# State stage of an audio tower: the cap of the inverse decays and the zeroing of first decays move from VectorE to GpSimd

## The chip, the cores and the metric

The kernel runs on one core of a Trainium2 chip. The metric is the device time in microseconds (us) of one execution; the time of a kernel is the median of several runs. Lines named L1033 and so on are lines of the kernel before.

## The reference, cut to what matters

The model takes 32 sequences of 750 samples with 64 channels and cuts each into 92 patches of 128 features (2944 tokens in all). Then follow a state space layer with a memory read-out, a mixture of six experts, a windowed attention and a second mixture. The change lies in the state space layer:

```python
delta = jnp.minimum(jax.nn.softplus(x_ssm @ delta_W + delta_b), 0.5)
A_cont = -jnp.exp(A_log)
DeltaA = delta[..., None] * A_cont
A_bar = jnp.clip(jnp.exp(DeltaA), 0.0, 1.0)
injection = jnp.where(jnp.abs(A_cont) > 0.0001, jnp.expm1(DeltaA) / A_cont, delta[..., None])
B_cont = jax.nn.silu(x_ssm @ B_W + B_b).reshape(Bsz, Tlen, d_h, n)
B_cont = 0.5 * (B_cont - jnp.mean(B_cont, axis=(0, 1), keepdims=True))
B_bar = jnp.nan_to_num(injection * B_cont, nan=0.0, posinf=1000.0, neginf=-1000.0)
A_shift = jnp.concatenate([jnp.ones((Bsz, 1, d_h, n), x_seq.dtype), A_bar[:, :-1]], axis=1)
pps = jnp.exp(jnp.cumsum(jnp.log(jnp.maximum(A_shift, 1e-06)), axis=1))
h_seq = jnp.cumsum(B_bar * pps, axis=1) / pps
C_coeff = jax.nn.silu(x_ssm @ C_W + C_b).reshape(Bsz, Tlen, d_h, n)
h_out = jnp.einsum('btdn,btdn->btd', h_seq, C_coeff)
```

There are 128 channels with 16 states each. The cumulative sum divided by the cumulative product is a recurrence, h[t] = h[t-1] / A_shift[t] + B_bar[t], and that is how the kernel computes it. The inverse decay 1 / A_shift is the growing exponential of the delayed delta, capped at 1e6, the inverse of the lower bound 1e-6; at the first token of a sequence it is set to zero, so that one scan can run over all 32 sequences.

## The kernel before, in words

The kernel has five stages. In each, every engine runs an instruction list of its own, the lists meet at semaphores, and every stage ends with all engines waiting for each other. The order of the work on each engine is written out by hand.

The second stage, the state stage, handles the 16 states one after another, in eight pairs (`NPAIR`). All its large tiles are 128 channels by `TOK` = 2944 tokens, `L` = 92 tokens to a sequence. Two slots u = 0 and 1 alternate for the buffers `bufB`, `bufC`, `th` and `ra`; `ea` exists once. For state n:

- ScalarE, `decays` (L745 on): `tanh` (L751) of half the decay's exponent into `th`; `exp_minus` (L756), the falling exponential, into `ea`; `exp_plus` (L761), the growing one, into `ra`. `exp_plus` of state n waits until the scan of state n-2 has released `ra` in its slot (`ra_free`). The order of a pair is tanh, exp_minus, exp_plus, tanh, exp_plus, exp_minus.
- TensorE, `states` (L1539 to L1541): the projections B and C of the state, three passes for each of eight banks of PSUM, 48 matmuls a state. The eight banks hold either B or C, so each group of banks must be emptied before the next can be filled.
- ScalarE, `silus`: the B group (L784) empties the banks into `bufB` and sums for the mean; the C group (L791) empties them into `bufC`. Before a C group it waits until the transfer of the state two before, which reads the same `bufC`, has landed (`Y_added`).
- VectorE, `injection` (L1028): `(ea + 1) * th`. `decay` (L1033, L1035): the cap of `ra` at 1e6 and the memset of every 92nd column to zero. `drive` (L1045, L1047, L1049): the mean of B, then `(B - mean) * th` into `bufB`. `recur` (L1054): the scan over `ra` and `bufB`. `read_out` (L1059): h times C into `bufC`. `weights_lo` (L1039), once a pair: the low part of the next weights.
- GpSimd, `add_state` (L601): a transfer that adds `bufC` to `Y` in place, for states 0 to 13; GpSimd then waits until it has landed. TensorE adds states 14 and 15.

VectorE's order in a pair is drive, scan, read_out of the first state, weights_lo, drive and scan of the second; then injection and decay for the first state of the next pair, read_out of the second, injection and decay for the second state of the next pair. SyncE loads the weights of each pair. The ScalarE side of the hand-over is:

```python
def exp_plus(n, u):
    wait_apart(act, ra_free, n + 1)
    act.activation(ra[:, u], dl[:, 0:TOK], ACT.Exp, scale=A_pos[:, bass.ds(n, 1)])\
        .then_inc(ra_ready, 1)
```

and the wait of a C group for the transfer:

```python
if not first:
    act.wait_ge(Y_added, 16 * n - 16)
```

Of the kernel before, what the change touches and what calls it, by code (L numbers as in the profile page):

```python
# [7 lines left out]
def audio_tower(nc, t, out):  # L8
# [11 lines left out]
    ALU = mybir.AluOpType  # L20
# [3 lines left out]
    B, L, D = out.shape  # L24
# [4 lines left out]
    TOK = B * L  # L29
    G = L + 1  # L30
    NS = 16
# [30 lines left out]
    with ctx:  # L62
# [3 lines left out]
        def sem(name):  # L66
            return ctx.enter_context(nc.semaphore(name))
# [48 lines left out]
        def take(*shape, parts=128):  # L116
            n = 1
            for s in shape:
                n *= s
            view = R[0:parts, taken[0]:taken[0] + n]  # L120
            taken[0] += n
            assert taken[0] <= R_COLS
            if len(shape) > 1:
                ax = "abcd"[:len(shape)]
                view = view.rearrange("p (" + " ".join(ax) + ") -> p " + " ".join(ax),
                                      **{x: s for x, s in zip(ax, shape)})
            return view
# [19 lines left out]
        def wait_apart(eng, s, value):  # L147


            eng.wait_ge(s, value)  # L150
            eng.sem_inc(apart, 1)
# [23 lines left out]
        def stage_end(eng, k):  # L175

            eng.drain().then_inc(stage_done, 1)  # L177
            eng.wait_ge(stage_done, 4 * k)
# [126 lines left out]
        ra = take(2, TOK)  # L305
        dl = take(1 + TOK)
        wBC = sb("wBC", [128, 2, 2, D])
        NPAIR = NS // 2
# [15 lines left out]
        Y_zero, Y_added = sem("Y_zero"), sem("Y_added")  # L324
        th_ready, ea_ready, ra_ready = sem("th_ready"), sem("ea_ready"), sem("ra_ready")
        th_free, ea_free, ra_free = sem("th_free"), sem("ea_free"), sem("ra_free")
        B_free = sem("B_free")
        prod_ready = sem("prod_ready")
        skip_mm = sem("skip_mm")

# [229 lines left out]
        def _(pool):  # L560
            step = Tally(pool, pool_step)
# [34 lines left out]
            pool.memset(Y[:, :], 0.0).then_inc(Y_zero, 1)  # L596
            pool.wait_ge(Y_zero, 1)

            def add_state(n, u):
                wait_apart(pool, prod_ready, n + 1)  # L600
                pool.dma_start(Y[:, :], bufC[:, u], accum_op=ALU.add, max_dma_last_dim=TOK // 2 * 4)\  # L601
                    .then_inc(Y_added, 16)
                pool.wait_ge(Y_added, 16 * n + 16)

            with pool.Fori(0, NPAIR - 1) as i:
                for u in range(2):
                    add_state(i * 2 + u, u)
            stage_end(pool, 2)

            def rstd_c(c):  # L610
# [318 lines left out]
        def _(dve):  # L929
            step = Tally(dve, dve_step)  # L930
# [93 lines left out]
            def injection(n, u):  # L1024

                dve.wait_ge(th_ready, n + 1)
                dve.wait_ge(ea_ready, n + 1)
                dve.scalar_tensor_tensor(th[:, u], ea, 1.0, th[:, u], ALU.add, ALU.mult).then_inc(ea_free, 1)  # L1028

            def decay(n, u):  # L1030

                dve.wait_ge(ra_ready, n + 1)
                step.add(dve.tensor_scalar(ra[:, u], ra[:, u], 1e6, None, ALU.min))  # L1033
                step.wait()
                step.add(dve.memset(ra[:, u, 0:TOK:L], 0.0))  # L1035

            def weights_lo(i, s):
                dve.wait_ge(w_hi_ready, i + 1)
                dve.tensor_tensor(w_lo[:, s], wBC[:, :, :, :], w_hi[:, s].bitcast(f32), ALU.subtract)\  # L1039
                    .then_inc(w_split, 1)  # L1040

            def drive(n, u):

                dve.wait_ge(bc_free, NH + (n * 2 + 1) * NH)
                step.add(dve.reduce_sum(mean[:, u:u + 1], part[:, u, :], axis=AX))  # L1045
                step.wait()
                step.add(dve.tensor_scalar(mean[:, u:u + 1], mean[:, u:u + 1], 1.0 / TOK, None, ALU.mult))  # L1047
                step.wait()
                dve.scalar_tensor_tensor(bufB[:, u], bufB[:, u], mean[:, u:u + 1], th[:, u],  # L1049
                                         ALU.subtract, ALU.mult).then_inc(th_free, 1)  # L1050

            def recur(n, u):
                dve.wait_ge(th_free, 2 + n + 1)
                dve.tensor_tensor_scan(bufB[:, u], ra[:, u], bufB[:, u], 0.0, ALU.mult, ALU.add).then_inc(ra_free, 1)  # L1054

            def read_out(n, u):
                dve.wait_ge(ra_free, 2 + n + 1)
                dve.wait_ge(bc_free, NH + (n * 2 + 2) * NH)
                step.add(dve.scalar_tensor_tensor(bufC[:, u], bufB[:, u], A_c[:, bass.ds(n, 1)], bufC[:, u],  # L1059
                                                  ALU.mult, ALU.mult))  # L1060
                step.wait()
                dve.sem_inc(B_free, 1)
                dve.sem_inc(prod_ready, 1)  # L1063

            def pair(i, s, more=True, weights=True):
                n = i * 2
                drive(n, 0)
                recur(n, 0)
                read_out(n, 0)
                if weights:  # L1070
                    weights_lo(i + 1, s)
                drive(n + 1, 1)
                recur(n + 1, 1)
                if more:
                    injection(n + 2, 0)
                    decay(n + 2, 0)
                read_out(n + 1, 1)
                if more:
                    injection(n + 3, 1)
                    decay(n + 3, 1)  # L1080

            dve.sem_inc(w_split, 1)
            weights_lo(0, 0)
            injection(0, 0)
            decay(0, 0)
            decay(1, 1)
            injection(1, 1)
            pair(0, 1)
            for i in step.loop(NPAIR // 2 - 1, 2 * (2 * 2 + 2 * 3)):
                pair(i * 2 + 1, 0)  # L1090
                pair(i * 2 + 2, 1)
            pair(NPAIR - 1, 0, False, False)
# [832 lines left out]
```

## Time and profile before

| what | value |
|---|---|
| median of 3 runs | 988.57 us (987.64 to 989.6) |
| the profiled execution's own time | 989.3 us |
| its span in the profile | 987.4 us |
| busy: TensorE, VectorE, ScalarE, GpSimd | 686.1, 673.5, 489.3, 279.8 us |
| state stage, VectorE busy from 113 to 432 us | 292.84 of 319.00 us |
| state stage, ScalarE busy from 113 to 432 us | 265.97 of 319.00 us |
| TensorE's granted clock from 148.85 to 378.52 us | 0.76 of full speed |

The profile counts an engine as busy while an instruction of its executes. Register, branch and semaphore instructions don't count. In brackets behind a row of the timeline stands how long the engine had been idle before the instruction, and what released it. [...]

### The profile page before, as it was taken

To read this page: it belongs to the slowest core of one execution; us is meant where nothing else is said; L and a number is where in the kernel's file an instruction comes from. 1 tells how busy PE (TensorE), PEld (TensorE's weight loads), DVE (VectorE), ACT (ScalarE), POOL (GpSimd) and SP (SyncE) were. 2 spreads that over 40 slices of the span, in tenths; PEclk is the share of its full clock that TensorE was granted. 3 is DMA by queue.
4 is the path that set the end of the run, shared out by engine and by line. 5 is a ranking of instruction groups with operands and counts; after the bars stand their busy time and mean duration, and the time that the engine had idled before them with its cause. 6 is when DMAs were issued, how large, how long until landed. Compare 5 with 4: busy or idle time off the path is not lost. (4 is left out here: it accounts for less than half of the span.)

```text
span 987.4 us, 12125 instructions
## 1 busy us (share of the span) xinstructions
PE 686.1 (69%) x3064; PEld 510.5 (52%) x3065; DVE 673.5 (68%) x1482; ACT 489.3 (50%) x691; POOL 279.8 (28%) x266
## 2 busy tenths in 40 slices
PE   6964253663753753856424993669999799999986
PEld 3542253563752743734322772346666566666654
DVE  0886379999999999968831442656857567675641
ACT  1234799889888988603211331234534344453432
POOL 0343101000000000002872442144352515445342
PEclk9995677877876777878556996779989989998999
DMA  4300425533543553316011211000000000000000
GB/s 163 128 5 0 160 72 98 107 61 79 109 77 72 96 98 61 61 34 229 22 34 32 60 54 56 22 0 1 9 1 8 2 8 0 8 9 0 8 3 14
DMA packets 22412, 50.97 MB, mean 52 GB/s; under 512 B 4485, under 2 KB 14704, under 8 KB 22016
## 3 DMA queue, kind: packets, MB, share of 16 engines
q0 software_dynamic: 6752, 24.53, 12.7%
q1 hardware_dynamic: 15616, 25.96, 8.4%
q8 instruction: 15, 0.25, 0.1%
q14 instruction: 29, 0.24, 0.1%
HBM read 24.44 MB, written 10.10 MB: 35 GB/s over the span
## 5 line engine op out<-in xcount | busy, mean ns | idle before, releaser
L1539 PE MATMUL psum<-s_xn_lo,s_split_hi 128*128 128x368 f32 x256 | 100.5, 393 | 148.0 <-ACT s_R L784 100.4
L1539 PEld LDWEIGHTS psum<-s_xn_lo,s_split_hi 128*128 128x128 f32 x256 | 59.1, 231 | 153.6 <-ACT s_R L784 102.8
L880 ACT ACTIVATE s_R<-psum,s_cols 128x368 f32<-128x368 f32 x96 | 54.2, 571 | 120.2 <-PE psum L1710 114.7
L1716 PE MATMUL psum<-s_R 128*128 128x368 f32 (+1 forms) x288 | 106.6, 491 | 0.0
L1054 DVE TENSOR_TENSOR_SCAN s_R<-s_R 128x2944 f32<-128x2944 f32 x16 | 100.7, 6291 | 0.6
L1540 PE MATMUL psum<-s_xn_hi,s_split_lo 128*128 128x368 f32 x256 | 96.9, 379 | 0.0
L1541 PE MATMUL psum<-s_xn_hi,s_split_hi 128*128 128x368 f32 x256 | 96.3, 376 | 0.0
L601 POOL DMA_DIRECT2D s_xnfm<-s_R x14 | 17.1, 1218 | 270.9 <-DVEq L1063 270.9
L1708 PE MATMUL psum<-s_xn_lo,s_split_hi 128*128 128x368 f32 (+1 forms) x144 | 78.7, 547 | 1.2 <-ACT s_R L880 0.9
L662 POOL TENSOR_TENSOR s_R<-s_R 128x368 f32<-128x368 f32 x48 | 46.5, 968 | 86.8 <-DVE s_R L1332 82.5
L1422 DVE TENSOR_TENSOR s_R<-psum,s_R 128x344 f32<-128x344 f32 x168 | 37.5, 280 | 44.4 <-PE psum L1782 42.1
L1716 PEld LDWEIGHTS psum<-s_R 128*128 128x128 f32 (+1 forms) x288 | 53.6, 195 | 25.4 <-issue 1.4
L791 ACT ACTIVATE s_R<-psum,s_cols 128x736 f32<-128x736 f32 x64 | 55.7, 877 | 14.9 <-PE psum L1541 10.3
L1540 PEld LDWEIGHTS psum<-s_xn_hi,s_split_lo 128*128 128x128 f32 x256 | 59.0, 230 | 0.0
L685 POOL TENSOR_TENSOR s_R<-s_R 128x368 f32<-128x368 f32 x48 | 46.5, 968 | 43.1 <-DVE s_R L1422 34.1
L1541 PEld LDWEIGHTS psum<-s_xn_hi,s_split_hi 128*128 128x128 f32 x256 | 58.2, 227 | 0.0
L1028 DVE SCALAR_TENSOR_TENSOR s_R<-s_R 128x2944 f32<-128x2944 f32 x16 | 51.4, 3214 | 9.2 <-ACT s_R L756 6.9
L784 ACT ACTIVATE s_R<-psum,s_cols 128x736 f32<-128x736 f32 x64 | 55.7, 876 | 2.3 <-PE psum L1541 1.2
L1059 DVE SCALAR_TENSOR_TENSOR s_R<-s_R,s_A_c 128x2944 f32<-128x2944 f32 x16 | 52.6, 3285 | 2.1 <-DVE s_R L1054 1.3
L1049 DVE SCALAR_TENSOR_TENSOR s_R<-s_R,s_mean 128x2944 f32<-128x2944 f32 x16 | 52.6, 3285 | 0.6
L1740 PE MATMUL psum<-s_R 128*112 128x368 f32 x112 | 45.7, 500 | 7.0 <-DVE s_R L1361 6.6
L761 ACT ACTIVATE s_R<-s_R,s_A_pos 128x2944 f32<-128x2944 f32 x16 | 43.9, 2742 | 13.0 <-DVE s_R L1054 13.0
(228 smaller groups left out, 1623.2 us busy)
## 6 DMA issues: line engine op xcount, KB each, us to landing
s_xnfm<-s_R POOLq DMA_DIRECT2D x14, 1472.0 KB, 10.5
s_R<-in_xg SPq DMA_DIRECT2D x8, 744.0 KB, 4.2
x_sorted<-in_x_init SPq DMA_DIRECT2D x1, 5082.0 KB, 18.7
s_R<-in_w SPq DMA_DIRECT2D x2, 1536.0 KB, 9.8
s_wBC<-in_wBC SPq DMA_DIRECT2D x8, 256.0 KB, 2.8
s_R<-x_sorted SPq DMA_DIRECT2D x28, 66.0 KB, 1.8
s_R<-y_rows SPq DMA_DIRECT2D x8, 184.0 KB
out<-s_R SPq DMA_DIRECT2D x8, 184.0 KB
```

The costliest lines, as they stand in the source:

```text
L784: act.activation(group(bufB, u, h), psum[:, h * HB:(h + 1) * HB, 0:CT], ACT.Silu, bias=cols[:, bass.ds(n + at["B_b"], 1)], scale=1.0, accu ...
L791: act.activation(group(bufC, u, h), psum[:, h * HB:(h + 1) * HB, 0:CT], ACT.Silu, bias=cols[:, bass.ds(n + at["C_b"], 1)], scale=1.0).then ...
L880: act.activation(fh[0:kk, e % 3, j], bank(j % 2 if e % 2 == 0 else (j + 1) % 2, kk), ACT.Gelu, bias=col("b1", 2 * e + j) if j < 2 else b1b ...
L1028: dve.scalar_tensor_tensor(th[:, u], ea, 1.0, th[:, u], ALU.add, ALU.mult).then_inc(ea_free, 1)
L1049: dve.scalar_tensor_tensor(bufB[:, u], bufB[:, u], mean[:, u:u + 1], th[:, u], ALU.subtract, ALU.mult).then_inc(th_free, 1)
L1054: dve.tensor_tensor_scan(bufB[:, u], ra[:, u], bufB[:, u], 0.0, ALU.mult, ALU.add).then_inc(ra_free, 1)
L1059: step.add(dve.scalar_tensor_tensor(bufC[:, u], bufB[:, u], A_c[:, bass.ds(n, 1)], bufC[:, u], ALU.mult, ALU.mult))
L1539: pe.matmul(bank(c), w_hi[:, s, u, k, :], xn_lo[:, a:b], start=True, stop=False)
L1540: pe.matmul(bank(c), w_lo[:, s, u, k, :], xn_hi[:, a:b], start=False, stop=False)
L1541: ins = pe.matmul(bank(c), w_hi[:, s, u, k, :], xn_hi[:, a:b], start=False, stop=True)
L1708: pe.matmul(o, w_hi_, fm(xn_lo, f), start=True, stop=False)
L1716: ins = pe.matmul(bank((2, 4)[e % 2]), w, fh[0:kk, e % 3, j], start=(j == 0), stop=(j == FT - 1))
```

## The change

VectorE's `decay` is gone. GpSimd gets `cap`: it waits for ScalarE's `exp_plus`, caps `ra` in place with a minimum at 1e6 and a maximum at 0.0, waits for that instruction, and sets every 92nd column to zero. VectorE's `recur` waits for the memset through the new semaphore `ra_capped`. On GpSimd the caps of the next pair stand between the transfer of a pair's first state and that of its second. GpSimd no longer waits for the landing behind each transfer but ahead of the next one, and once for all at the end.

```diff
             pool.memset(Y[:, :], 0.0).then_inc(Y_zero, 1)
             pool.wait_ge(Y_zero, 1)
 
-            def add_state(n, u):
+            def add_state(n, u, first=False):
                 wait_apart(pool, prod_ready, n + 1)
+                if not first:
+                    wait_apart(pool, Y_added, 16 * n)
                 pool.dma_start(Y[:, :], bufC[:, u], accum_op=ALU.add, max_dma_last_dim=TOK // 2 * 4)\
                     .then_inc(Y_added, 16)
-                pool.wait_ge(Y_added, 16 * n + 16)
-
-            with pool.Fori(0, NPAIR - 1) as i:
-                for u in range(2):
-                    add_state(i * 2 + u, u)
+
+            def cap(n, u):
+
+                wait_apart(pool, ra_ready, n + 1)
+                pool.tensor_scalar(ra[:, u], ra[:, u], 1e6, 0.0, ALU.min, ALU.max).then_inc(ra_capped, 1)
+                wait_apart(pool, ra_capped, 2 * n + 1)
+                pool.memset(ra[:, u, 0:TOK:L], 0.0).then_inc(ra_capped, 1)
+
+            cap(0, 0)
+            cap(1, 1)
+            add_state(0, 0, True)
+            cap(2, 0)
+            cap(3, 1)
+            add_state(1, 1)
+            with pool.Fori(1, NPAIR - 1) as i:
+                add_state(i * 2, 0)
+                cap(i * 2 + 2, 0)
+                cap(i * 2 + 3, 1)
+                add_state(i * 2 + 1, 1)
+            pool.wait_ge(Y_added, 16 * (NS - 2))
             stage_end(pool, 2)
...
-            def decay(n, u):
-
-                dve.wait_ge(ra_ready, n + 1)
-                step.add(dve.tensor_scalar(ra[:, u], ra[:, u], 1e6, None, ALU.min))
-                step.wait()
-                step.add(dve.memset(ra[:, u, 0:TOK:L], 0.0))
-
...
             def recur(n, u):
+                dve.wait_ge(ra_capped, 2 * n + 2)
                 dve.wait_ge(th_free, 2 + n + 1)
...
                 if more:
                     injection(n + 2, 0)
-                    decay(n + 2, 0)
                 read_out(n + 1, 1)
                 if more:
                     injection(n + 3, 1)
-                    decay(n + 3, 1)
 
             dve.sem_inc(w_split, 1)
             weights_lo(0, 0)
             injection(0, 0)
-            decay(0, 0)
-            decay(1, 1)
             injection(1, 1)
             pair(0, 1)
-            for i in step.loop(NPAIR // 2 - 1, 2 * (2 * 2 + 2 * 3)):
+            for i in step.loop(NPAIR // 2 - 1, 2 * (2 * 3)):
```

## Rows read from the trace of the kernel before

**Rows 1.** Timeline of VectorE: start us, us, line, operation, out<-in
```profile
148.85 0.15 DVE L1045 TENSOR_REDUCE s_mean<-s_part 128x1 f32<-128x4 f32 x1
...
235.36 3.20 DVE L1028 SCALAR_TENSOR_TENSOR s_R<-s_R 128x2944 f32<-128x2944 f32 x1
238.48 1.69 DVE L1033 TENSOR_SCALAR s_R<-s_R 128x2944 f32<-128x2944 f32 x1
...
240.43 3.29 DVE L1059 SCALAR_TENSOR_TENSOR s_R<-s_R,s_A_c 128x2944 f32<-128x2944 f32 x1
...
249.46 0.16 DVE L1045 TENSOR_REDUCE s_mean<-s_part 128x1 f32<-128x4 f32 x1 [0.40 <-ACT s_R L791]
...
378.52 0.15 DVE L1045 TENSOR_REDUCE s_mean<-s_part 128x1 f32<-128x4 f32 x1
```

**Rows 2.** VectorE over six pairs: stretch, its length, busy us (instructions), clock, DMA
```profile
148.85:378.52 229.67, 219.91 (x103) 0.76 0.45 86
```

**Rows 3.** Groups of VectorE, 148.85 to 378.52 us: busy us, mean ns | idle before
```profile
L1054 DVE TENSOR_TENSOR_SCAN s_R<-s_R 128x2944 f32<-128x2944 f32 x12 | 75.5, 6291 | 0.4
...
L1028 DVE SCALAR_TENSOR_TENSOR s_R<-s_R 128x2944 f32<-128x2944 f32 x12 | 38.5, 3212 | 2.0 <-DVE s_R L1059 2.0
L1033 DVE TENSOR_SCALAR s_R<-s_R 128x2944 f32<-128x2944 f32 x12 | 20.2, 1686 | 0.0
...
L1035 DVE MEMSET s_R<- 128x32 f32 x12 | 1.0, 85 | 1.2
```

**Rows 4.** Groups of ScalarE over the same six pairs
```profile
L756 ACT ACTIVATE s_R<-s_R,s_A_neg 128x2944 f32<-128x2944 f32 x13 | 35.8, 2753 | 1.9 <-DVE s_R L1028 1.8
...
L761 ACT ACTIVATE s_R<-s_R,s_A_pos 128x2944 f32<-128x2944 f32 x12 | 32.9, 2743 | 10.4 <-DVE s_R L1054 10.4
```

**Rows 5.** GpSimd's transfers: the timeline, and the page's list of issues
```profile
244.45 1.19 POOL L601 DMA_DIRECT2D s_xnfm<-s_R  x1 [17.98 <-DVEq L1063]
...
s_xnfm<-s_R POOLq DMA_DIRECT2D x14, 1472.0 KB, 10.5
```

**Rows 6.** Groups of GpSimd over the whole execution: busy us, mean ns | idle before
```profile
L685 POOL TENSOR_TENSOR s_R<-s_R 128x368 f32<-128x368 f32 x48 | 46.5, 968 | 43.1 <-DVE s_R L1422 34.1 <-POOL s_R L685 9.1
...
L225 POOL TENSOR_SCALAR s_pa<-s_mv 92x4 f32<-92x4 f32 x16 | 3.1, 191 | 77.9 <-DVE s_mv L205 77.9
L596 POOL MEMSET s_xnfm<- 128x2944 f32 x1 | 2.6, 2552 | 9.6 <-DVEq L177 9.6
...
L620 POOL COPY s_R<-s_R 92x128 f32<-92x128 f32 x1 | 0.3, 312 | 43.6 <-DMA s_R<-in_tile_rest 43.6
```

**Rows 7.** VectorE's two-input L1361 and GpSimd in the last stage: source view, timelines
```profile
L1361 DVE TENSOR_TENSOR s_R<-s_R x56: 498/505/1594, 619.9 to 916.4; 128x344 f32<-128x344 f32 x56
...
619.88 3.07 DVE L1361 TENSOR_TENSOR s_R<-s_R 128x344 f32<-128x344 f32 x7
...
740.22 2.21 POOL L672 TENSOR_TENSOR s_R<-s_R 4x11 f32<-4x11 f32 x1 [0.59 <-DVE s_R L1348]
740.37 5.24 DVE L1361 TENSOR_TENSOR s_R<-s_R 128x344 f32<-128x344 f32 x7
...
742.40 1.55 POOL L677 TENSOR_TENSOR s_H<-s_H,s_rows 92x512 f32 x1
...
870.77 5.20 POOL L672 TENSOR_TENSOR s_R<-s_R 4x11 f32<-4x11 f32 x1 [0.59 <-DVE s_R L1348]
...
870.93 3.06 DVE L1361 TENSOR_TENSOR s_R<-s_R 128x344 f32<-128x344 f32 x7
```

**Rows 8.** Timeline of ScalarE in one pair: exponentials, end of the B group, next C group
```profile
235.63 2.75 ACT L761 ACTIVATE s_R<-s_R,s_A_pos 128x2944 f32<-128x2944 f32 x1 [1.25 <-DVE s_R L1054]
238.75 2.75 ACT L756 ACTIVATE s_R<-s_R,s_A_neg 128x2944 f32<-128x2944 f32 x1 [0.37 <-DVE s_R L1028]
...
246.66 0.21 ACT L784 ACTIVATION_READ_ACCUMULATOR s_R<-psum,s_cols 128x1 f32 x1
...
256.42 3.83 ACT L791 ACTIVATE s_R<-psum,s_cols 128x736 f32<-128x736 f32 x4
```

More of the change, by code:

```diff
@@ L327, in audio_tower @@
         B_free = sem("B_free")
+        ra_capped = sem("ra_capped")
         prod_ready = sem("prod_ready")
```

## The prediction

> **What bounds the kernel now.** The change touches the state stage alone (16 states, some 113 to 432 us), so I read that stretch engine by engine. VectorE is its bound. One pair of states takes the time from one start of the mean's reduction to the same one of the next pair: from 148.85 to 378.52 us there are six pairs [rows 1], so 229.67 / 6 = 38.28 us each, of which VectorE is busy 219.91 / 6 = 36.65 [rows 2]. The rest, 1.6 us, is short gaps, most of them a wait for its own semaphore. The costly operations are the scan (6.29 us) and three fused ones of about 3.2 us per state; the cap and the memset that leave it take 1.69 and 0.09 us [rows 3].
>
> ScalarE is next. In the same six pairs it waits 10.4 us before the growing exponential for VectorE's scan and 1.9 us before the falling one, 1.8 of it for the injection [rows 4]; so it would need 38.28 - (10.4 + 1.8) / 6 = 36.25 us per pair if VectorE never held it up. That figure contains its waits for TensorE. GpSimd only issues the accumulating transfers, every 19 us, each landing some 10.5 us after issue [rows 5].
>
> **What is removed.** On VectorE the cap starts at 238.48 and the read-out behind the memset at 240.43 [rows 1]: 1.95 us with the gaps, 3.90 per pair. Pairs 0 to 6 contain such a turn of two caps, so seven pairs count. The caps of states 0 and 1 stand before the first pair, where VectorE waits for ScalarE anyway; I cost them at nothing. If that cover were gone, they would cost what one pair's do. The counts of semaphore steps in the loop are bookkeeping and cost nothing.
>
> **What is added.** Sixteen caps of 128x2944 on GpSimd, sixteen memsets of 32 strided columns, three waits. The trace has no such cap. From below: a memset of the same 2944 columns, which reads nothing, took 2.55 us. From above: the two-input sum took 968 ns for 368 columns; with 191 ns for the 4-column operation as its fixed part that is 2.13 ns a column, 6.5 us for 2944. Nearest is the one-input operation: 312 ns for 128 columns less the same 191 for 4 gives 0.98 ns a column, hence 191 + 2940 x 0.98 = 3.06 us [rows 6]. I take 3.06, because the cap reads one tensor and the constants are in the instruction. The small memset writes 32 elements; the one on VectorE took 0.09 us [rows 3], I take 0.1 to 0.3 and hide it behind VectorE's next operation, which doesn't wait for it.
>
> [...]
>
> **Does GpSimd's cap run beside VectorE?** This decides. The trace shows it in the last stage. Seven VectorE multiplications with both inputs in SBUF take 3.07 us when GpSimd is idle, but 5.24 us when GpSimd runs an operation of 2.21 us and one of 1.55 us across them. One of these multiplications reaches 1594 ns where the median is 505. In another chunk the seven take 3.06 us, and then it is GpSimd's small operation, just issued, that takes 5.20 us in place of 2.21 and ends 1.98 us after the last of the seven [rows 7]. So a GpSimd operation that reads SBUF and a two-input operation of VectorE do not run together: one waits, sometimes the one, sometimes the other. After the change nearly everything long on VectorE in this stage has two inputs in SBUF: the drive, the scan, the injection and the read-out. There is nowhere to put 2 x 3.06 us beside it, unless VectorE idles.
>
> [...]
>
> **The sum.** I lay out one pair from the drive of its first state at 0. That drive's reduction starts at 249.46 - 38.28 = 211.18 us, the injection behind the second scan at 235.36 [rows 1], so the second scan ends at 24.2; the injection, 3.2 us, follows.
> - If GpSimd gets in as soon as VectorE's current instruction ends, the cap of state n+2 (input ready from ScalarE before the scan ends) runs right after the scan, and the cap of n+3 right after the injection. Both delay VectorE in full: 38.28 - 3.90 + 2 x 3.06 = 40.50 us a pair.
> - If VectorE's back-to-back stream keeps GpSimd out until a gap, the caps start in the 0.3 us gap behind a read-out and at the two tiny mean operations (0.15 each) before a drive; this hides 0.6 us: 39.9.
>
> ScalarE's and the mixed loop stay below: from a drive's start to the second scan's end is 24.2, and from the growing exponential at 235.63 to the last accumulator read of the B group at 246.66 + 0.21 it is 11.2 [rows 8], with hand-overs about 36. A cap ahead of the injection makes this 24.2 + 3.06 + 3.2 + 0.3, then 8.1 from the falling exponential at 238.75 to the same read: 38.9, with the last hand-over 39.1, still under 40.5. I take the middle, 40.2, that is +1.9 a pair (40.2 - 38.28) and 7 x 1.9 = +13.3 us for the stage. Nothing overlaps the stage's end, so it goes through whole.
>
> **The transfers.** Moving GpSimd's wait for the landing to the next issue gains nothing where transfers of 10.5 us are issued 19 us apart. But behind the cap of n+3 on GpSimd's queue stands the transfer of state n+1, and ScalarE's C group of state n+3 waits for it. Before, it was issued at 244.45 [rows 5] and the group began at 256.42 [rows 8], with about a microsecond to spare. In the second layout the cap of n+3 ends some 6 us later than the read-out needs, so ScalarE stalls up to 6 us there. ScalarE's own need is 36.25 against a pair of 39.9 and it catches up before the drive after the next, with about 2 us left. I cost it at nothing; if the cap took 5 us or more, this chain could set the pair.
>
> The profiled execution took 989.3 us around a span of 987.4, 0.7 above the median of 988.57. 989.3 + 13.3 = 1002.6; for a median I say 1002.
>
> **Rivals.**
> 1. No contention: the caps hide. For it: not all overlaps in the last stage are slow, and no row shows this conflict for a fused operation or a scan. Then VectorE needs 38.28 - 3.90 = 34.4, ScalarE sets the pair at 36.25, and 7 x 2.03 = 14.2 us go: 975. This ends on the other side; it decides wherever a cap delays VectorE by under 1.95 us. Chance 0.15.
> 2. Partial conflict: the delay is 2.17 / 3.76 = 0.58 of GpSimd's time. Then 2 x 3.06 x 0.58 = 3.5 replaces 3.9, -0.35 a pair, about 987. The two cases of fully blocked instructions speak against it. Chance 0.08, split between faster and same.
> 3. Dear caps: a software minimum and maximum may cost nearer to the two-input row. At 6.5 us: 34.4 + 13 = 47.4, +9.1 a pair, 1053; at 4.3 us, +4.7, 1022. Chance 0.09.
>
> The forecast itself has 0.68. With caps of 2.55 us and the full hiding it gives 38.28 - 3.90 + 5.1 - 0.6 = 38.9, +0.6 a pair, 993; with 4 us and no hiding 42.4, +4.1, 1018. The range reaches from 985, which takes in rival 2, to 1022, the lower half of rival 3; it leaves out rival 1 and the rest of rival 3, 0.2 together. A measurement here tells apart about 0.2%, 2 us: faster 0.15 + 0.05, same 0.05 with the edge of the forecast's low end, slower the rest, 0.75.
>
> **What the profile after would show.** Right: L1033 and L1035 gone from VectorE, the removed 27 us of their seven pairs replaced by longer means of the fused operations or the scan, by one cap's length each time, or by idle time before the scan; GpSimd's cap rows of about 3 us, or up to 9 us where it waits inside its span; a pair of 39.9 to 40.5; ScalarE idling more for VectorE. Wrong: the fused operations still at 3.2 us and the scan at 6.29 beside a running cap, a pair near 36.3 and ScalarE without waits for the scan; that is rival 1. Caps of over 4 us with VectorE idle before the scan would be rival 3. If ScalarE's C group waits long for the transfer and VectorE then waits for ScalarE, the chain I cost at nothing has failed.

## The result, and the profile after

The kernel after takes 992.62 us (median of 8 runs, 991.23 to 994.6) against 987.81 us of the kernel before in the same series: a ratio of 1.0048, 95% interval 1.0032 to 1.0064. It is slower by some 4.8 us. The forecast was +13.3 us and 1002; the way was right, the size was not.

The timeline of VectorE in a middle pair of the kernel after, with lines of that kernel (L1046 injection, L1056 and L1058 mean, L1060 drive, L1066 scan, L1071 read-out); columns as in [rows 1]:

```profile
225.87 0.15 DVE L1056 TENSOR_REDUCE s_mean<-s_part 128x1 f32<-128x4 f32 x1
...
229.56 6.29 DVE L1066 TENSOR_TENSOR_SCAN s_R<-s_R 128x2944 f32<-128x2944 f32 x1
235.77 5.59 DVE L1046 SCALAR_TENSOR_TENSOR s_R<-s_R 128x2944 f32<-128x2944 f32 x1
241.28 5.65 DVE L1071 SCALAR_TENSOR_TENSOR s_R<-s_R,s_A_c 128x2944 f32<-128x2944 f32 x1
247.27 3.23 DVE L1046 SCALAR_TENSOR_TENSOR s_R<-s_R 128x2944 f32<-128x2944 f32 x1 [0.33 <-DVE s_R L1071]
...
381.74 0.15 DVE L1056 TENSOR_REDUCE s_mean<-s_part 128x1 f32<-128x4 f32 x1
```

GpSimd in the same stretch (L610 the cap, L612 the memset, L604 the transfer):

```profile
233.21 5.07 POOL L610 TENSOR_SCALAR s_R<-s_R 128x2944 f32<-128x2944 f32 x1 [6.17 <-ACT s_R L779]
238.44 0.16 POOL L612 MEMSET s_R<- 128x32 f32 x1 [0.15 <-POOL s_R L610]
238.98 4.88 POOL L610 TENSOR_SCALAR s_R<-s_R 128x2944 f32<-128x2944 f32 x1 [0.38 <-ACT s_R L779]
...
247.84 1.22 POOL L604 DMA_DIRECT2D s_xnfm<-s_R  x1 [3.66 <-DVEq L1075]
```

The reader is to see three things. The cap and the memset, 1.95 us each time with gaps [rows 1], are gone from VectorE. In their place the injection takes 5.59 us instead of 3.20, and the read-out 5.65 instead of 3.29: 2.39 and 2.36 us more. And the caps are recorded with 5.07 and 4.88 us, though the second in the prologue, with VectorE idle, took 2.64:

```profile
125.46 2.64 POOL L610 TENSOR_SCALAR s_R<-s_R 128x2944 f32<-128x2944 f32 x1 [1.97 <-ACT s_R L779]
```

The first cap is issued at 233.21, in the middle of the scan, and ends at 238.28, 2.43 us after the scan's end at 235.85. So it waited for the scan, and then the injection waited for it. A pair takes (381.74 - 225.87) / 4 = 38.97 us against 38.28 before: +0.69 in seven pairs is 4.8 us. That this is the difference of the medians to the tenth is partly luck. From the second mean of the stage to the last, over all seven pairs, the traces have 419.89 - 147.54 = 272.35 us against 415.71 - 148.85 = 266.86, which is 5.5 us, as the first pair and the last grow more than those between; the interval of the ratio is 3.2 to 6.3 us.

### The profile page after: what moved, and what is told of

It is laid out like the page before. It is cut to its first block and busy times, and to the rows that moved or that the text cites. A ratio compares the mean times of both kernels' runs of the same rounds, so it can differ in the third digit from the quotient of the medians.

```text
span 992.7 us, 12186 instructions
## 1 busy us (share of the span) xinstructions
PE 690.1 (70%) x3064; PEld 513.3 (52%) x3065; DVE 678.9 (68%) x1450; ACT 488.5 (49%) x691; POOL 359.1 (36%) x298
## 5 line engine op out<-in xcount | busy, mean ns | idle before, releaser
L1066 DVE TENSOR_TENSOR_SCAN s_R<-s_R 128x2944 f32<-128x2944 f32 x16 | 100.7, 6291 | 0.8
L610 POOL TENSOR_SCALAR s_R<-s_R 128x2944 f32<-128x2944 f32 x16 | 76.2, 4759 | 57.5 <-ACT s_R L779 57.5
L1046 DVE SCALAR_TENSOR_TENSOR s_R<-s_R 128x2944 f32<-128x2944 f32 x16 | 68.2, 4260 | 15.7 <-ACT s_R L774 13.4
L1071 DVE SCALAR_TENSOR_TENSOR s_R<-s_R,s_A_c 128x2944 f32<-128x2944 f32 x16 | 69.1, 4319 | 1.5 <-DVE s_R L1066 1.2
L604 POOL DMA_DIRECT2D s_xnfm<-s_R x14 | 17.2, 1231 | 139.6 <-DVEq L1075 139.6
L774 ACT ACTIVATE s_R<-s_R,s_A_neg 128x2944 f32<-128x2944 f32 x16 | 44.0, 2749 | 19.4 <-DVE s_R L1046 19.3
L1060 DVE SCALAR_TENSOR_TENSOR s_R<-s_R,s_mean 128x2944 f32<-128x2944 f32 x16 | 52.6, 3285 | 0.9 <-DVE s_mean L1058 0.3
```

The source lines that it names most:

```text
L610: pool.tensor_scalar(ra[:, u], ra[:, u], 1e6, 0.0, ALU.min, ALU.max).then_inc(ra_capped, 1)
```

## The experiments

Pairs are measured as above, from a mean's reduction to the same one of a later pair, over four or five pairs behind the first. The kernel before has 38.27 over four of these pairs and 38.23 over five. The ratios are those to the kernel before in runs on the same chip.

**Whether reading matters on GpSimd's side.**

```diff
-                pool.tensor_scalar(ra[:, u], ra[:, u], 1e6, 0.0, ALU.min, ALU.max).then_inc(ra_capped, 1)
+                pool.memset(ra[:, u], 0.0).then_inc(ra_capped, 1)
```

> The changed kernel with GpSimd's cap replaced by a memset of the same 2944 columns, so GpSimd works as long but reads nothing; the decays are all zero, so the recurrence is left out. Theory A (a GpSimd instruction that READS SBUF and a two-input VectorE instruction exclude each other): injection and read-out back to 3.2 and 3.3 us in every pair, VectorE needs 34.4 us a pair, ScalarE sets the pair at about 36.3, some 14 us below the kernel before, about 974 us. Theory B (any GpSimd access to SBUF blocks VectorE, reading or writing): each memset of 2.55 us still costs some 2.3 us, pair near 38.9, about 992 us. Theory C (the time of the changed kernel comes from the new waits and the order on GpSimd's queue, not from a conflict): also about 992 us, with VectorE's operations at 3.2 us and idle time instead.

971.02 us, ratio 0.9817 (0.9801 to 0.9833), pair 35.96. The timelines of VectorE and GpSimd:

```profile
224.65 6.29 DVE L1066 TENSOR_TENSOR_SCAN s_R<-s_R 128x2944 f32<-128x2944 f32 x1
230.86 3.20 DVE L1046 SCALAR_TENSOR_TENSOR s_R<-s_R 128x2944 f32<-128x2944 f32 x1
233.97 3.28 DVE L1071 SCALAR_TENSOR_TENSOR s_R<-s_R,s_A_c 128x2944 f32<-128x2944 f32 x1
...
228.90 2.54 POOL L610 MEMSET s_R<- 128x2944 f32 x1 [6.77 <-ACT s_R L779]
...
234.17 2.56 POOL L610 MEMSET s_R<- 128x2944 f32 x1 [2.42 <-ACT s_R L779]
```

Memsets of 2.55 us run right across the scan and the read-out, and neither side is lengthened: the scan stays at 6.29 us, the injection at 3.20, the read-out at 3.28. It is GpSimd's reading that conflicts here; B and C fall.

**Whether reading matters on VectorE's side.**

```diff
-                dve.scalar_tensor_tensor(th[:, u], ea, 1.0, th[:, u], ALU.add, ALU.mult).then_inc(ea_free, 1)
+                dve.reduce_sum(unused[:, 1:2], ea, axis=AX).then_inc(ea_free, 1)
```

> The changed kernel with the injection replaced by a sum over ea, a VectorE instruction of about the same length with one input in SBUF (the product with th is left out). Theory A: the cap that now stalls the injection runs beside the sum, which stays near 3.2 us; only the read-out is stalled, so 38.97 - 2.4 = 36.6 us a pair, or ScalarE's 36.3 to 36.6, about 976 us. If it doesn't matter how many inputs VectorE reads, the sum takes 5.6 us and the kernel stays near 992 us.

971.96 us, ratio 0.9821 (0.9795 to 0.9847), pair 35.87. The timelines of VectorE and GpSimd, L1046 now the sum:

```profile
226.72 6.29 DVE L1066 TENSOR_TENSOR_SCAN s_R<-s_R 128x2944 f32<-128x2944 f32 x1
232.93 3.19 DVE L1046 TENSOR_REDUCE s_unused<-s_R 128x1 f32<-128x2944 f32 x1
236.04 3.27 DVE L1071 SCALAR_TENSOR_TENSOR s_R<-s_R,s_A_c 128x2944 f32<-128x2944 f32 x1
239.64 3.22 DVE L1046 TENSOR_REDUCE s_unused<-s_R 128x1 f32<-128x2944 f32 x1 [0.33 <-DVE s_R L1071]
...
230.37 5.08 POOL L610 TENSOR_SCALAR s_R<-s_R 128x2944 f32<-128x2944 f32 x1 [6.17 <-ACT s_R L779]
...
236.14 5.68 POOL L610 TENSOR_SCALAR s_R<-s_R 128x2944 f32<-128x2944 f32 x1 [0.38 <-ACT s_R L779]
```

The first cap ends at 235.45, 2.44 us after the scan's end at 233.01: it waited for the scan as before, and then ran beside the one-input sum, which stays at 3.19 us. The second waited for the read-out and ran beside the next sum. I had expected the read-out to be stalled still; with the sum as cover for both caps nothing is. So in these runs this conflict came only with two inputs on VectorE and a read on GpSimd: the injection takes 5.59 us beside the reading cap, 3.20 beside a memset, and the one-input sum 3.19 beside the reading cap.

**The cost doubled.** GpSimd caps twice, the second after the first (the counts of `ra_capped` become 3 a state).

```diff
                 pool.tensor_scalar(ra[:, u], ra[:, u], 1e6, 0.0, ALU.min, ALU.max).then_inc(ra_capped, 1)
-                wait_apart(pool, ra_capped, 2 * n + 1)
+                wait_apart(pool, ra_capped, 3 * n + 1)
+                pool.tensor_scalar(ra[:, u], ra[:, u], 1e6, 0.0, ALU.min, ALU.max).then_inc(ra_capped, 1)
+                wait_apart(pool, ra_capped, 3 * n + 2)
```

> The changed kernel with each cap done twice in a row on GpSimd, the second after the first's semaphore. Theory A: each further cap stalls one VectorE instruction by 2.4 us, 4.8 us a pair, pair near 43.8 and the kernel near 1026 us; some of the stalls may fall on the scan or the drive, which no run has shown lengthened yet. If the caps were hidden and the changed kernel lost its time elsewhere (theory C): GpSimd's queue has room for 5 us more a pair, so near 993 us.

1027.06 us, ratio 1.0377 (1.0362 to 1.0392), pair (412.22 - 235.91) / 4 = 44.08. The timeline of VectorE in the third pair, one of 42.96 us, shows four instructions lengthened by 2.4, 2.0, 2.0 and 2.3 us, the scan among them (L1048 injection, L1062 drive, L1068 scan, L1073 read-out):

```profile
205.97 5.66 DVE L1073 SCALAR_TENSOR_TENSOR s_R<-s_R,s_A_c 128x2944 f32<-128x2944 f32 x1
211.96 5.24 DVE L1048 SCALAR_TENSOR_TENSOR s_R<-s_R 128x2944 f32<-128x2944 f32 x1 [0.34 <-DVE s_R L1073]
...
217.49 5.29 DVE L1062 SCALAR_TENSOR_TENSOR s_R<-s_R,s_mean 128x2944 f32<-128x2944 f32 x1
222.81 8.62 DVE L1068 TENSOR_TENSOR_SCAN s_R<-s_R 128x2944 f32<-128x2944 f32 x1
```

From the fourth pair on, in the pairs of 44.08, it looks otherwise:

```profile
246.91 3.23 DVE L1048 SCALAR_TENSOR_TENSOR s_R<-s_R 128x2944 f32<-128x2944 f32 x1 [1.02 <-ACT s_R L776]
250.05 5.66 DVE L1073 SCALAR_TENSOR_TENSOR s_R<-s_R,s_A_c 128x2944 f32<-128x2944 f32 x1
257.46 3.82 DVE L1048 SCALAR_TENSOR_TENSOR s_R<-s_R 128x2944 f32<-128x2944 f32 x1 [1.76 <-ACT s_R L776]
262.75 0.16 DVE L1058 TENSOR_REDUCE s_mean<-s_part 128x1 f32<-128x4 f32 x1 [1.46 <-ACT s_R L804]
263.14 3.71 DVE L1062 SCALAR_TENSOR_TENSOR s_R<-s_R,s_mean 128x2944 f32<-128x2944 f32 x1
266.89 8.61 DVE L1068 TENSOR_TENSOR_SCAN s_R<-s_R 128x2944 f32<-128x2944 f32 x1
```

The stalls are 2.4, 0.6, 0.4 and 2.3 there, 5.7 us a pair and not four times 2.4, and VectorE waits 4.2 us for ScalarE. The total came out as expected, but not all of it by stalls: the waits for transfers grew too, 150 to 430 us:

```profile
ACT s_R L811 <- DMA s_xnfm<-s_R: 58.1, 6, 11.1
```

Four caps ahead of a transfer make ScalarE's C group wait 58.1 us in six places. That the number met the expectation is partly luck: two causes of similar size, of which I had named one.

**The caps taken out.** What a free cap would give.

```diff
-                pool.tensor_scalar(ra[:, u], ra[:, u], 1e6, 0.0, ALU.min, ALU.max).then_inc(ra_capped, 1)
-                wait_apart(pool, ra_capped, 2 * n + 1)
                 pool.memset(ra[:, u, 0:TOK:L], 0.0).then_inc(ra_capped, 1)
...
-                dve.wait_ge(ra_capped, 2 * n + 2)
+                dve.wait_ge(ra_capped, n + 1)
```

> The changed kernel without any cap; GpSimd does only the memset of 32 columns. Left out: the minimum at 1e6. Theory A: VectorE's chain falls to 34.4 us a pair, ScalarE's own need of 36.25 becomes the pair, about 974 us; this is what the move would have given if the cap had been free. Theory C: still about 992 us.

971.47 us, ratio 0.9827 (0.9811 to 0.9842), pair 35.90. VectorE now waits for ScalarE's B group before each pair's first drive, and ScalarE's two exponentials still wait a little for VectorE's injection and scan; the waits, 150 to 400 us:

```profile
DVE s_mean L1054 <- ACT s_R L800: 10.5, 7, 1.6
...
ACT s_R L772 <- DVE s_R L1044: 1.6, 5, 0.4
...
ACT s_R L777 <- DVE s_R L1064: 1.1, 3, 0.4
```

So all other parts of the change together, queue and waits included, leave the full gain. Only the cap takes it back.

**Only the memset moved.** The cap stays on VectorE behind GpSimd's memset.

```diff
-                pool.tensor_scalar(ra[:, u], ra[:, u], 1e6, 0.0, ALU.min, ALU.max).then_inc(ra_capped, 1)
-                wait_apart(pool, ra_capped, 2 * n + 1)
                 pool.memset(ra[:, u, 0:TOK:L], 0.0).then_inc(ra_capped, 1)
...
+            def decay(n, u):
+
+                dve.wait_ge(ra_capped, n + 1)
+                step.add(dve.tensor_scalar(ra[:, u], ra[:, u], 1e6, None, ALU.min))
```

(`decay` is called where the kernel before calls it, and `recur` doesn't wait for GpSimd.)

> The cap goes back to VectorE, only the memset of the 32 first columns stays on GpSimd, ahead of the cap (GpSimd waits for ScalarE, VectorE's cap for the memset). Theory A: a small write reads nothing and costs VectorE nothing, while the memset (0.09 us), its wait for the cap and the gap go: 1.95 - 1.69 = 0.26 us a state, 3.6 us over seven pairs, about 984 us, faster than both kernels. Theory B: the memset of 0.16 us stalls VectorE about as long as it saved, near 988 us.

982.92 us, ratio 0.9932 (0.9918 to 0.9947), pair 37.41. And once more beside the changed kernel:

> The kernel with only the memset on GpSimd once more, beside the changed kernel: 0.4 to 0.7% below the kernel before, 4 to 7 us, and about 1% below the changed kernel.

982.24 us, ratio 0.9919 (0.989 to 0.9947), pair 37.41. This version is below both kernels, twice. The timelines of VectorE (L1049 the cap) and GpSimd show it:

```profile
238.46 1.68 DVE L1049 TENSOR_SCALAR s_R<-s_R 128x2944 f32<-128x2944 f32 x1
240.06 3.28 DVE L1073 SCALAR_TENSOR_TENSOR s_R<-s_R,s_A_c 128x2944 f32<-128x2944 f32 x1
...
232.39 0.15 POOL L610 MEMSET s_R<- 128x32 f32 x1 [5.77 <-ACT s_R L777]
238.52 1.72 POOL L610 MEMSET s_R<- 128x32 f32 x1 [5.98 <-ACT s_R L777]
```

From the cap's start to the read-out's it is 1.60 us, before 1.95. That is 0.35 a state; the rest of 38.28 - 37.41 = 0.87 a pair is mostly the gap of 0.40 ahead of the mean [rows 1], which is gone. The kernel before has this gap in every second pair only, 0.2 us a pair; its waits, 150 to 412 us:

```profile
DVE s_mean L1045 <- ACT s_R L791: 1.3, 3, 0.6
```

I had expected 0.26 a state. The second memset takes 1.72 us in place of 0.15: issued just after VectorE's cap began, it ends at 240.24, as that one has ended; the same goes for six of these memsets in the first trace and for six in the second (1.5 to 1.7 us). So the fast one-input cap (1.69 us for 2944 columns, where injection and read-out take 3.20 and 3.28) does hold up a GpSimd write, here by some 1.6 us. Nothing waits for that memset here.

**Only the wait in GpSimd's queue moved.** Cap and memset stay on VectorE.

```diff
-            def add_state(n, u):
+            def add_state(n, u, first=False):
                 wait_apart(pool, prod_ready, n + 1)
+                if not first:
+                    wait_apart(pool, Y_added, 16 * n)
                 pool.dma_start(Y[:, :], bufC[:, u], accum_op=ALU.add, max_dma_last_dim=TOK // 2 * 4)\
                     .then_inc(Y_added, 16)
-                pool.wait_ge(Y_added, 16 * n + 16)
...
```

(The first two transfers stand ahead of the loop, and GpSimd waits once for all landings at the end, as in the change.)

> The kernel before with only GpSimd's wait for the landing moved ahead of the next transfer; cap and memset stay on VectorE. Both theories: transfers of 10.5 us issued 19 us apart, so no change, within 2 us of the kernel before. If it moved by more, that part of the change has an effect of its own.

988.66 us, ratio 0.9989 (0.9967 to 1.001), pair 38.23, the same as before over these five: no effect.

**Half of the caps moved.** Even states as in the change, odd ones as before.

```diff
             cap(0, 0)
-            cap(1, 1)
             add_state(0, 0, True)
             cap(2, 0)
-            cap(3, 1)
             add_state(1, 1)
             with pool.Fori(1, NPAIR - 1) as i:
                 add_state(i * 2, 0)
                 cap(i * 2 + 2, 0)
-                cap(i * 2 + 3, 1)
                 add_state(i * 2 + 1, 1)
...
```

(`decay` stays on VectorE for the odd states, and `recur` waits for GpSimd at the even ones only.)

> Cap and memset on GpSimd for the even states only, on VectorE for the odd ones. Theory A: a pair is 38.28 - 1.95 + 2.4 = 38.7 at most, half of what the whole change cost, so +2 to +3 us on the kernel before, about 990 us. A theory in which the first cap uses up slack and only the second one costs would put it at or below the kernel before.

994.41 us, ratio 1.0034 (1.0006 to 1.0062), pair 38.72 against 38.23 over the same five. Over all seven pairs it is 418.68 - 148.42 = 270.26 us, 3.4 more than before: the first cap costs at once, there is no slack for it. But the median lies 5.5 us above that of the kernel before (988.95), and so above the 990 that I had expected; the ratio gives 3.4 us, with runs that scatter on both sides. In the profiled execution, of 996.15 us, what the stage doesn't explain lies behind it: from the end of the last addition of the skip to the end of the kernel it takes 553.8 us, against 549.5 in the kernel before and 546.4 to 550.7 in all others of this document, though the code there is the same. Why, no run shows. The finding rests on the pairs, not on the median.

**Each cap in two halves.**

```diff
-                pool.tensor_scalar(ra[:, u], ra[:, u], 1e6, 0.0, ALU.min, ALU.max).then_inc(ra_capped, 1)
-                wait_apart(pool, ra_capped, 2 * n + 1)
+                pool.tensor_scalar(ra[:, u, 0:TOK // 2], ra[:, u, 0:TOK // 2], 1e6, 0.0, ALU.min, ALU.max).then_inc(ra_capped, 1)
+                pool.tensor_scalar(ra[:, u, TOK // 2:TOK], ra[:, u, TOK // 2:TOK], 1e6, 0.0, ALU.min, ALU.max).then_inc(ra_capped, 1)
+                wait_apart(pool, ra_capped, 3 * n + 2)
...
```

> The changed kernel with each cap as two GpSimd instructions of 1472 columns, neither waiting for the other. Theory A with the lock held for one instruction: VectorE is stalled by the same 2.4 us in all, in one piece or in two, plus some 0.1 to 0.2 us for the second instruction: pair 39.0 to 39.4, the kernel 992 to 996 us. If shorter instructions slip into VectorE's gaps, the stall falls and so does the time, at most by 0.3 us a cap, to about 988 us.

987.19 us, ratio 0.9969 (0.9944 to 0.9994), pair 38.52. The first of my expectations, 992 to 996, missed. The second, about 988, nearly has the number, but the reason is another one than a stall that slips into small gaps. GpSimd's timeline, L610 and L611 being the halves, and the largest wait of ScalarE:

```profile
235.88 4.07 POOL L610 TENSOR_SCALAR s_R<-s_R 128x1472 f32<-128x1472 f32 x1 [9.13 <-ACT s_R L780]
240.03 4.27 POOL L611 TENSOR_SCALAR s_R<-s_R 128x1472 f32<-128x1472 f32 x1
...
244.69 3.96 POOL L610 TENSOR_SCALAR s_R<-s_R 128x1472 f32<-128x1472 f32 x1
248.73 1.42 POOL L611 TENSOR_SCALAR s_R<-s_R 128x1472 f32<-128x1472 f32 x1
...
ACT s_R L810 <- DMA s_xnfm<-s_R: 24.0, 6, 4.9
```

A half takes 1.41 us alone, but in the pair shown three of the four are recorded with 3.96 to 4.27 and end some 1.27 us after the VectorE instruction beside them, and so the four take 14 us a pair. The transfer behind them is late, ScalarE's C groups wait 24.0 us for transfers, and VectorE idles for ScalarE; some halves run in that idle time for nothing. The seven pairs take 416.85 - 148.48 = 268.37 us, 1.5 more than before, so they are no gain. 2.4 us of the difference lie at the stage's end. From the last read-out's end to the end of the last addition of the skip it is 430.24 to 436.69, 6.45 us, against 429.03 to 437.91, 8.88 us, in the kernel before. TensorE's last matmuls there, and its stretch 428 to 437 us (length, busy, clock), first the kernel before, then this one:

```profile
416.78 5.11 PE L1554 MATMUL psum<-s_R,s_ident 128*128 128x368 f32 x16
429.24 7.65 PE L1554 MATMUL psum<-s_R,s_ident 128*128 128x368 f32 x16 [7.35 <-DVEq L1063]
...
428.00:437.00 9.00, 7.65 (x16) 0.66 0.00 0
```

```profile
425.30 10.37 PE L1563 MATMUL psum<-s_R,s_ident 128*128 128x368 f32 x32
...
428.00:437.00 9.00, 7.63 (x24) 1.00 0.00 0
```

Here the C group was so late that TensorE had no pause in front of its last sixteen matmuls, and the granted clock is 1.00 of full speed over the stretch: 32 of these matmuls take 10.37 us. In the kernel before it is idle for 7.35 us, the granted clock is 0.50 from 425 to 434 us, and the last sixteen take 7.65 us at a mean clock of 0.68, where the sixteen ahead of the pause took 5.11 at 1.00. That is 2.5 us, the size of the difference. The rest of what parts this kernel from the one before is within the interval.

**The two queue orders.** In both, the transfer of a pair's second state goes ahead of the cap of the next pair's second state.

```diff
...
-                cap(i * 2 + 3, 1)
                 add_state(i * 2 + 1, 1)
+                cap(i * 2 + 3, 1)
```

With the halves:

> The two-halves kernel with the transfer of a pair's second state ahead of the cap of the next pair's second state on GpSimd's queue. The two-halves kernel waited 24 us for transfers in ScalarE's C groups, which left VectorE idle, and some of the half caps ran in that idle time. Theory A: the waits for transfers go, VectorE's idle time goes too, so the four half caps of a pair stall it by 1.15 us each less the gap of 0.3: 38.28 - 3.90 + 4.3 = 38.7 a pair against 38.42 with the waits, so 989 to 992 us: no gain, though a wait of 24 us is gone. If the transfers' wait sets the pair of the two-halves kernel, it falls towards 36.3 and some 975 us.

989.97 us, ratio 0.9998 (0.9977 to 1.0018), pair 38.39. The waits of the C groups for transfers are gone from the list of waits, and the pair falls by 0.13 only; the halves now stall the scan too (mean 6.77 us). (The 38.42 in the expectation is the pair with the waits over four pairs; 38.52 is over five.)

With whole caps:

> The changed kernel, caps whole, with the same reordering of GpSimd's queue. Theory A: the cap of the first state still stalls the injection by 2.4 us; that of the second starts behind the transfer's issue, gets in at the tiny mean operations and stalls the drive by about 2.1: 38.28 - 3.90 + 4.5 = 38.9 a pair, the same as the changed kernel within 1 us. If the queue order cost the changed kernel its time, it falls by 5 us or more.

989.21 us, ratio 0.999 (0.9965 to 1.0015), pair 38.58: 0.39 below the changed kernel, 2.7 us, between the two expectations. The timelines of VectorE and GpSimd show why it is not nothing:

```profile
244.51 3.23 DVE L1046 SCALAR_TENSOR_TENSOR s_R<-s_R 128x2944 f32<-128x2944 f32 x1 [0.33 <-DVE s_R L1071]
249.32 0.16 DVE L1056 TENSOR_REDUCE s_mean<-s_part 128x1 f32<-128x4 f32 x1 [1.58 <-ACT s_R L802]
...
249.71 3.59 DVE L1060 SCALAR_TENSOR_TENSOR s_R<-s_R,s_mean 128x2944 f32<-128x2944 f32 x1
...
246.38 3.85 POOL L610 TENSOR_SCALAR s_R<-s_R 128x2944 f32<-128x2944 f32 x1
```

The second cap falls into 1.58 us in which VectorE waits for ScalarE, and stalls the drive by 0.3 us instead of 2.1. The first cap's stall sets the pair now, by way of ScalarE: it delays the injection, on which the falling exponential and then the B group hang, and for the B group VectorE's mean waits. The waits, 150 to 400 us:

```profile
ACT s_R L774 <- DVE s_R L1046: 18.2, 7, 2.8
DVE s_mean L1056 <- ACT s_R L802: 9.5, 6, 1.6
```

This is the mixed loop of the prediction. It stood there at 38.9 with a cap of 3.06; with 2.39 it is 38.2, and with the 0.3 of the drive and the hand-overs it comes to the 38.58. So the changed kernel's pair lies only 0.4 to 0.7 us above its second bound: there ScalarE ends the B group at 249.67, and VectorE comes to the mean at 250.41.

**The change itself again.**

> The changed kernel itself, beside the others on one chip: 0.4 to 0.6% above the kernel before, some 5 us.

992.48 us, ratio 1.0027 (1.0004 to 1.005), pair 38.97: the same pair to the hundredth, and the same 272.35 us over the seven. The ratio is below the expected 0.4%, though its interval reaches 0.5%. In this series the kernel before scattered more (984.63 to 996.86), hence the wide interval; the first ratio is the better one.

## Why the prediction was wrong

**What fell: the price of one cap.** The step "I take 3.06" is the one that failed. The line through the copy and the 4-column operation [rows 6] gave 3.06 us; a cap that finds VectorE idle takes 2.64, near the memset, 2.55, which I had as the lower end. On top of that, VectorE loses less than the cap's record: 2.36 to 2.39 us, as the cap's record ends 2.43 us after the scan's: its first 0.2 us seem to overlap the instruction in front of it, which is argued from these ends and not tested. With 2.38 my own sum reads 38.28 - 3.90 + 2 x 2.38 = 39.14 a pair; measured were 38.97, and the 0.17 between them is the gap of 0.40 ahead of the mean, which the kernel before has in every second pair and the changed one in none between 150 and 412 us. With 3.06 the sum read 40.50. The net of a cap is the small difference of 2.38 and 1.95, so an error of 0.68 in the price more than doubled the forecast: 15.5 us with 3.06, 6.0 with 2.38, 4.8 without the gap. That a cap is paid in full, the 2 x 3.06 in the sum, was my estimate too: [rows 7] gave a delay of 5.24 - 3.07 = 2.17 us for 2.21 + 1.55 = 3.76 us of GpSimd work, 0.58 of it. No run shows a VectorE instruction delayed by 3.06 us for one cap; in the kernel after it is 2.36 to 2.39.

**What fell besides: the middle of two layouts.** Of the two layouts the first held in all fourteen caps of the seven pairs: the pending cap gets in as soon as VectorE's current instruction ends. Seven injections and seven read-outs are lengthened, no scan and no drive. The hiding of 0.6 us a pair, which I had mixed in, didn't occur. It took 2 us off the forecast, so this mistake, by luck, brought it nearer. The low end of the forecast itself, 38.9 a pair and 993 us with caps of 2.55 and the full hiding, meets the measurement for a wrong reason as well: the stall was shorter than the memset's 2.55, and nothing was hidden.

**What held.** The bound: VectorE sets the pair, and the loop through both engines is next, 0.4 to 0.7 us below. The caps of states 0 and 1 at nothing: from ScalarE's first exponential of the stage to the first mean it is 21.4 us in both kernels (113.30 to 134.66 before, 111.96 to 133.31 after). The half-moved kernel shows that no slack stood in front. The conflict: it came with a GpSimd read (in the write-only run the injection and the read-out are at 3.20 and 3.28 us) and with two inputs on VectorE (in the one-input run the sum is at 3.19). The two hardly overlap: a stall of 2.38 us for a cap of 2.64, 0.90 of it, not the 0.58 of rival 2; 0.26 us are missing to the whole cap. The wait in the queue: no effect, as said. The chain through the transfer: with whole caps ScalarE waits 1.0 us for transfers in the list of waits, so costing it at nothing was right; with longer work on GpSimd it does grow, to 24.0 and 58.1 us.

**The rivals.** Rival 1, no contention, is excluded, but its time was nearly right: with the cap out, or writing only, 971 us are measured where I gave 975. The pair of 35.9 there is not ScalarE's need of 36.25. Each engine waits for the other in it, so the loop through both sets it, which the prediction had put at 24.2 and 11.2, with hand-overs about 36. ScalarE's need by itself must be lower than 36.25; why, stays open. Its waits for TensorE didn't shrink (8.7 and 1.2 us over seven pairs, with the cap taken out as before). Rival 2 is excluded by the full stalls, rival 3 by the 2.64 us.

## What to carry to other kernels

In these runs an operation on GpSimd cost VectorE nothing only where the VectorE instruction beside it read one tensor from SBUF (the sum, 3.19 us beside a cap), or where GpSimd's only wrote (read-out 3.28 us beside a memset of 2.55); and a write on GpSimd was itself held up by VectorE's fast one-input cap (1.72 us in place of 0.15). Beside two-input instructions the balance is what the moved instruction stalls VectorE against what it took there, here 2.38 against 1.95 us. An operation that VectorE does fast, such as this cap of 1.69 us, therefore has the least to give; other operations were not tried. Move the memset and keep the cap: that was worth 0.7 to 0.8%.

When the gain is a difference of two similar prices, measure the new instruction by itself before forecasting; a price of 3.06 us, where VectorE lost 2.38, turned 5 us into 13.

## What the runs showed of the hardware that I had not expected

- A pending GpSimd read got in at the end of VectorE's current instruction in all fourteen cases of this stage (seven injections of 5.59 us, seven read-outs of 5.65), though VectorE's next one was queued right behind it. The case of [rows 7] in which seven VectorE instructions, 3.06 us in all, passed in front of a GpSimd one recorded with 5.20 didn't come back here.
- Shorter GpSimd instructions were not better at slipping in: a half of 1.41 us took up to 4.27, beside a read-out of 4.43 us, and ended 1.27 us after it.
- A GpSimd memset of 0.15 us took 1.72 beside VectorE's one-input cap, while a memset of 2.55 us was not lengthened beside two-input instructions. So the two conflicts did not come under the same conditions; whether VectorE's cap would be stalled by a GpSimd write already under way was not tried.
- Where TensorE had no pause of 7.35 us ahead of the stage's last sixteen matmuls, the stage's end was 2.4 us shorter, with a granted clock of 1.00 in place of 0.66 over the same 9 us. This is one comparison; no run changed the pause alone.
